# Layer norm's statistics of layer 0 worked out with tokens on partitions instead of on every partition

## The chip, the cores and the metric

The kernel runs on one core of a Trainium2 chip. The metric is the device time of one execution in microseconds (us). PE is the matrix engine, PEld its weight loads, DVE the vector engine, ACT the scalar engine, POOL the GpSimd engine, and SP issues DMAs.

## The reference

The input x is (2, 768, 64, 64) in float32. Two layers follow one another; the change touches layer 0 only, and in it only the layer norm over the 1536 channels of y.

```python
# layer 0
x_dbl = xs_seq @ x_proj_w.T                 # xs: in_proj, 3x3 depthwise conv, silu
dt, Bs, Cs = jnp.split(x_dbl, [R, R + DSTATE], axis=-1)
delta = softplus(einsum('blr,dr->bdl', dt, dt_w[0]) + dt_b)
# states: scan over tokens of dA = exp(delta * A), dBu = delta * u * Bs, 4 states a channel
y = jnp.einsum('bdln,bln->bdl', states, Cs) + D_param * u
mu = y.mean(-1, keepdims=True)
var = y.var(-1, keepdims=True)
y = (y - mu) * jax.lax.rsqrt(var + 1e-05) * ln_g + ln_b
out = y @ out_proj_w.T                      # then x = x + out
# layer 1: group norm, attention over statistics of w = x @ W_qkv.T, W_out, x = x + out
```

## The kernel before

Layer 0 keeps channels on partitions and tokens along the free dimension. The tokens of both images are cut into NCH = 16 chunks of N = 512 tokens (eight image rows each), and the 1536 channels into K = 12 tiles of P = 128. So there are NT = 192 pairs of chunk and tile. A loop over slots S = 0 to 213 is written out by hand for every engine: in slot S each engine does its share for tiles that entered the pipeline a fixed number of slots ago. A chunk takes 12 slots. In this document slots are counted modulo 12, so that in slot 8 the statistics of a chunk are worked out, and slot 0 is where a new chunk enters.

In slot S, PE multiplies tile S with the input weights (`in_proj`, L562, into bank p_in), and works on half of an output block of an older chunk (`out_proj`, L578, into bank p_op). In even slots it also sums y and y squared over channels with a matrix of ones (L633, L634, into the four quarters of p_ln). In every fourth slot it makes the inputs of softplus (`delta_pair`, L534, into p_dt), and in slots 1 and 2 the x_proj products (L667, also into p_dt). ACT moves p_in into the image window (L731), starts the convolution (L756), squares y (L762, which the sums of squares wait for) and writes the decays (L698) that DVE's scans need, two in the first half of a slot's work and two at the end of the slot before. DVE does four scans (L897), multiplies them by C (L907), adds six taps of the convolution (L922) and, in odd slots, scales and adds an output block (`scale_out` L929, `residual_add` L936, which sets s_ov and so lets PE use p_op again). POOL adds up and multiplies, and starts a DMA that adds two states onto two others (L851).

The order of the work on each engine is the order in which the loop's body issues it, and an engine goes on only when the wait at its head is met. Semaphores count: the name of the wait (s_ov, s_op, s_rstd, s_xd, s_delta, s_y) tells what is waited for. A matrix product of float32 with 512 columns shows as two passes in the trace.

For the norm, ACT copies the sums out of p_ln into LS at the end of slot 6 (L826): rows 0 to 63 hold the sums of squares, rows 64 to 127 the sums, each over 32 equal rows per quarter. At the end of slot 7, PE multiplies them with `pick`, a 128x128 matrix of one constant, so that the mean and the mean square of each token stand on all 128 partitions (L654, L656). In slot 8, ACT squares the mean (L744), DVE subtracts (L960) and adds epsilon (L962) between its first two times_c and its first tap, ACT takes Ln (L790) and Exp (L792) as a first guess of the root, and DVE does one Newton step in four operations after its last tap of the slot (L983, L985, L987, L989). All of these work on 128x512 values whose 128 rows are the same. The result RS is used by scale_out from slot 9 on. `norm_bank(c)` is p_dt, and p_da for the last chunk.

After the loop of the last chunk, PE still has two output blocks to do (`last_out_proj`, L608), DVE scales and adds the last six blocks (`scale_last`, `add_last`), and then layer 1 begins. The small operations of group norm (`group_norm_scale`, L66 to L101, values of 128x1) and layer 1's products with few columns (L1256) run on the same engines.

## Time and profile before

| | before |
|---|---|
| median of 3 runs (lowest to highest) | 3892.75 us (3892.51 to 3893.79) |
| the profiled execution: its time, its span | 3894.47 us, 3892.7 us |
| mean granted clock of PE, as a share of 2.4 GHz | 0.943 |
| PE busy, matrix products | 3479.1 us, 89% of the span, 10696 instructions |
| DVE busy | 2988.7 us, 77%, 4466 instructions |
| ACT busy | 2287.7 us, 59%, 3710 instructions |
| POOL busy | 2345.4 us, 60%, 1557 instructions |

Busy time is added over the whole span. Up to 81 us the kernel prepares weights and the first group norm; layer 0's loop runs from there to 2932 us, full from 484 us on; layer 1 takes the rest. An engine's share over the span therefore says little of any one stage. In the views, a bracket behind a row is the idle time of that engine just before it and the work that ended it.

### The profile page before, as it was taken

Reading aid. Unit: us, or ns where it says so; the run is one execution under the profiler, and the core shown is the slowest. Engines: PE = TensorE matmul, PEld = TensorE weight load, DVE = VectorE, ACT = ScalarE, POOL = GpSimd, SP = SyncE. Lnnn points to the kernel's source line nnn. Section 1 sums busy time; section 2 is a strip of 40 time slices with the busy share of each in tenths; the row PEclk is TensorE's granted clock in tenths of the full one; section 3 lists DMA queues with packets and bytes.
Section 4 is the critical chain, followed back from the end, with each engine's and each line's share of the span. In section 5 each row is a group of like instructions: output and inputs, shape, how many; then the busy total and the mean of one; then the engine's idle time right before and its main releaser. Section 6 shows DMA issues by size and latency. Waiting matters only on the chain. (4 is left out here: it accounts for less than half of the span.)

```text
span 3892.7 us, 39046 instructions
## 1 busy us (share of the span) xinstructions
PE 3479.1 (89%) x10696; PEld 1744.0 (45%) x10696; DVE 2988.7 (77%) x4466; ACT 2287.7 (59%) x3710; POOL 2345.4 (60%) x1557
## 2 busy tenths in 40 slices
PE   4875799999999899999989999998797999999999
PEld 4422233333333344333333333333245877767787
DVE  4459999999999979999999999999853345555532
ACT  1356767777777757776777777776534555432211
POOL 0138888888888868887888888888840001112211
PEclk7887899999999999999999999998898999999999
DMA  7234445545545544555555455554633223355654
GB/s 272 85 133 106 103 127 136 152 126 141 133 131 149 145 118 120 141 134 132 146 142 140 126 139 142 137 144 100 176 97 109 65 71 103 107 172 200 198 194 154
DMA packets 217034, 529.85 MB, mean 136 GB/s; under 512 B 24728, under 2 KB 45784, under 8 KB 213872
## 3 DMA queue, kind: packets, MB, share of 16 engines
q1 hardware_dynamic: 173808, 376.32, 30.5%
q0 software_dynamic: 43008, 151.02, 17.6%
q8 instruction: 88, 1.44, 0.1%
q14 instruction: 130, 1.06, 0.1%
HBM read 346.11 MB, written 80.48 MB: 110 GB/s over the span
## 5 line engine op out<-in xcount | busy, mean ns | idle before, releaser
L578 PE MATMUL p_op<-uy,wout_ring 128*128 128x512 f32 x2160 | 1060.0, 640 | 134.1 <-DVE x_res L936 134.0
L562 PE MATMUL p_in<-xn,win_v 128*128 128x512 f32 (+1 forms) x2304 | 1056.3, 609 | 76.7 <-ACT halo L735 43.4
L897 DVE TENSOR_TENSOR_SCAN p_da<-p_da,state,g_ring 128x512 f32<-128x512 f32 x672 | 827.3, 1277 | 121.2 <-ACT p_da L698 98.5
L869 POOL TENSOR_TENSOR g_ring<-du,B_bc 128x2048 f32<-128x2048 f32 x192 | 870.1, 4532 | 17.0 <-DMA B_bc<-bc_scratch 2.1
L922 DVE SCALAR_TENSOR_TENSOR p_cv<-win_v,conv_w,p_cv 128x512 f32<-128x512 f32 x960 | 722.9, 753 | 105.2 <-ACT p_cv L756 84.2
L578 PEld LDWEIGHTS p_op<-uy,wout_ring 128*128 128x128 f32 x2160 | 421.0, 203 | 771.3 <-issue 591.4
L562 PEld LDWEIGHTS p_in<-xn,win_v 128*128 128x128 f32 x2304 | 445.6, 197 | 657.4 <-issue 657.4
L698 ACT ACTIVATE p_da<-delta,A 128x512 f32<-128x512 f32 x768 | 496.8, 678 | 323.2 <-DVE g_ring L907 322.0
L907 DVE TENSOR_TENSOR g_ring<-p_da,C_bc 128x512 f32<-128x512 f32 x768 | 494.9, 686 | 1.1 <-issue 1.1
L1356 PE MATMUL banks<-x_split,w_split 128*128 128x512 f32 x1152 | 464.0, 403 | 24.9 <-DVE w_split L1536 19.7
L1358 PE MATMUL banks<-x_split,w_split 128*128 128x512 f32 x1152 | 451.7, 392 | 0.0
L1357 PE MATMUL banks<-x_split,w_split 128*128 128x512 f32 x1152 | 451.4, 392 | 0.0
L856 POOL TENSOR_TENSOR uy<-uy,conv_part 128x512 f32<-128x512 f32 x192 | 243.8, 1270 | 294.9 <-DVE uy L922 289.9
L1201 POOL DMA_DIRECT2D q_scratch<-q_ring x96 | 51.9, 540 | 537.5 <-DVE q_ring L1621 537.2
L851 POOL DMA_DIRECT2D g_ring<-g_ring x192 | 168.1, 876 | 193.3 <-DVE g_ring L907 185.0
L703 ACT ACTIVATE conv_part<-win_v,conv_w 128x512 f32<-128x512 f32 x384 | 274.1, 717 | 13.1 <-POOL uy L859 1.9
L1356 PEld LDWEIGHTS banks<-x_split,w_split 128*128 128x128 f32 x1152 | 217.7, 189 | 118.2 <-issue 39.4
L859 POOL TENSOR_TENSOR uy<-uy,conv_part 128x512 f32<-128x512 f32 x192 | 244.2, 1272 | 29.0 <-POOL uy L856 2.2
L877 POOL TENSOR_TENSOR uy<-uy,g_ring 128x512 f32<-128x512 f32 x192 | 243.8, 1270 | 15.1
L873 POOL TENSOR_TENSOR g_ring<-g_ring 128x512 f32<-128x512 f32 x192 | 243.8, 1270 | 10.8 <-DMA g_ring<-g_ring 10.8
L863 POOL TENSOR_TENSOR du<-delta,uy 128x512 f32<-128x512 f32 x192 | 248.5, 1294 | 2.0 <-ACT delta L717 2.0
L1358 PEld LDWEIGHTS banks<-x_split,w_split 128*128 128x128 f32 x1152 | 217.8, 189 | 47.4
(212 smaller groups left out, 4029.9 us busy)
## 6 DMA issues: line engine op xcount, KB each, us to landing
g_ring<-g_ring POOLq DMA_DIRECT2D x192, 512.0 KB, 5.2
win_v<-in_win SPq DMA_DIRECT2D x192, 384.0 KB, 3.2
wout_ring<-wout_scratch SPq DMA_DIRECT2D x184, 384.0 KB, 3.7
x_ring<-x_scratch SPq DMA_DIRECT2D x192, 256.0 KB, 2.7
q_scratch<-q_ring POOLq DMA_DIRECT2D x96, 256.0 KB, 2.4
x_split<-q_scratch SPq DMA_DIRECT2D x96, 256.0 KB, 3.2
out<-x_ring POOLq DMA_DIRECT2D x96, 256.0 KB, 2.8
x_res<-in_x SPq DMA_DIRECT2D x90, 256.0 KB, 4.2
```

The lines of the kernel that those rows point to most:

```text
L562: last = nc.tensor.matmul(p_in[:, 0:n], WR[:, i % NW, t, :], XN[:, t, off:off + n], start=(t == 0), stop=(t == XT - 1))
L578: last = nc.tensor.matmul(p_op[:], OR[:, e % NO, k - h * HALF, :], ucol(c * K + k), start=(k == 0), stop=(k == K - 1))
L698: nc.scalar.activation(p_da[:, n % 2, :], DL[:, i % ND, :], ACT.Exp, scale=At[:, j * NS + n:j * NS + n + 1]).then_inc(s_da, 1)
L703: nc.scalar.activation(rows(CT[:, n]), win_view(i, 2, 1 + n), ACT.Copy, scale=cwt[:, i % K, 7 + n:8 + n]).then_inc(s_ct, 1)
L863: nc.gpsimd.tensor_tensor(DU[:], DL[:, i % ND, :], ucol(i), ALU.mult).then_inc(s_du, 1)
L869: nc.gpsimd.tensor_tensor(G[:, i % NG], DU[:].unsqueeze(1).broadcast_to([P, NS, N]), BB[:], ALU.mult).then_inc(s_dbu, 1)
L897: nc.vector.tensor_tensor_scan(bank, bank, G[:, i % NG, n, :], init, ALU.mult, ALU.add)\
L907: nc.vector.tensor_tensor(G[:, i % NG, n], p_da[:, n % 2, :], CB[:, n], ALU.mult).then_inc(s_cm, 1)
L922: nc.vector.scalar_tensor_tensor(rows(dst), win_view(i, dy, dx), cwt[:, j, 3 * dy + dx:3 * dy + dx + 1], rows(p_cv[:]), ALU.mult, ALU.add) ...
L1356: nc.tensor.matmul(bank(m), WX[:, m, q, 0, :], hi(h), start=(q == 0), stop=False)
L1357: nc.tensor.matmul(bank(m), WX[:, m, q, 0, :], lo(h), start=False, stop=False)
L1358: last = nc.tensor.matmul(bank(m), WX[:, m, q, 1, :], hi(h), start=False, stop=(q == XT - 1))
```

## The change

The statistics are worked out with tokens on partitions. At the end of slot 7, PE now uses the sums LS as weights, 128 tokens at a time, and a `pick` of two columns as the moving operand: four products put the mean and the mean square of 512 tokens into 128x8 values. In slot 8, DVE copies them into `tst` (128 tokens by 4 blocks), squares, subtracts and adds epsilon in four operations; ACT takes Ln and Exp of 128x4; DVE does the four operations of the Newton step on 128x4, now ahead of the last three taps instead of behind them. At the end of slot 8, PE waits for the fourth of these and spreads the result: four products with `tst`'s column, repeated 128 times, as weights and the identity matrix `ident0` as moving operand write 1/sigma of 512 tokens to all 128 partitions. At the start of slot 9, ACT copies that into RS. ACT's Square is gone. `delta_pair` no longer waits for s_var. The identity matrix is loaded by one more DMA at the start, and `pick` is set by four small memsets instead of one.

```diff
-        pick = sb("pick", [P, P])
+        pick = sb("pick", [P, 2])
+        ident0 = sb("ident0", [P, P])
+        tst = sb("token_stats", [P, 8, N // P])
...
-                      (quad[:], g["quad_d"]), (fold[:], g["ident_d"]),
+                      (quad[:], g["quad_d"]), (fold[:], g["ident_d"]), (ident0[:], g["ident_d"]),
...
-                    wait(pe, s_var, norms_before(S))
                     wait(pe, s_rstd, norms_before(S))
...
-                        nc.tensor.matmul(norm_bank(c)[:, 0, :], pick[64:P, :], LS[64:P, :], start=True, stop=True)\
-                          .then_inc(s_mean, 1)
-                        nc.tensor.matmul(norm_bank(c)[:, 1, :], pick[0:64, :], LS[0:64, :], start=True, stop=True)\
-                          .then_inc(s_e2, 1)
+                        for tb in range(N // P):
+                            last = nc.tensor.matmul(norm_bank(c)[:, 0, 2 * tb:2 * tb + 2], LS[:, tb * P:(tb + 1) * P],
+                                                    pick[:], start=True, stop=True)
+                        last.then_inc(s_e2, 1)
+                    c = chunk_at(S, S_LN + 1)
+                    if c is not None:
+                        pe.wait_ge(s_nt, 4 * (c + 1))
+                        for tb in range(N // P):
+                            last = nc.tensor.matmul(norm_bank(c)[:, 1, tb * P:(tb + 1) * P],
+                                                    tst[:, 6, tb:tb + 1].broadcast_to([P, P]), ident0[:],
+                                                    start=True, stop=True)
+                        last.then_inc(s_rsb, 1)
...
-                    c = chunk_at(S, S_LN + 1)
+                    c = chunk_at(S, S_LN + 2)
                     if c is not None:
-                        act.wait_ge(s_mean, c + 1)
-                        act.wait_ge(s_e2, c + 1)
-                        nc.scalar.activation(LS[:], norm_bank(c)[:, 0, :], ACT.Square).then_inc(s_msq, 1)
+                        act.wait_ge(s_rsb, c + 1)
+                        wait(act, s_oa, XT * c)
+                        nc.scalar.activation(RS[:], norm_bank(c)[:, 1, :], ACT.Copy).then_inc(s_rstd, 1)
...
-                        nb = norm_bank(c)[:, 0, :]
-                        nc.scalar.activation(nb, LS[:], ACT.Ln).then_inc(s_lv, 1)
+                        nc.scalar.activation(tst[:, 4, :], tst[:, 3, :], ACT.Ln).then_inc(s_lv, 1)
                         act.wait_ge(s_lv, c + 1)
-                        nc.scalar.activation(nb, nb, ACT.Exp, scale=-0.5).then_inc(s_rs0, 1)
+                        nc.scalar.activation(tst[:, 4, :], tst[:, 4, :], ACT.Exp, scale=-0.5).then_inc(s_rs0, 1)
...
+                        st = norm_bank(c)[:, 0, 0:2 * (N // P)].rearrange("p (t s) -> p s t", s=2)
                         vec.wait_ge(s_e2, c + 1)
-                        vec.wait_ge(s_msq, c + 1)
-                        nb = norm_bank(c)
-                        nc.vector.tensor_tensor(nb[:, 1, :], nb[:, 1, :], LS[:], ALU.subtract).then_inc(s_var, 1)
-                        vec.wait_ge(s_var, c + 1)
-                        nc.vector.tensor_scalar(LS[:], nb[:, 1, :], 0.0, 1e-5, ALU.max, ALU.add).then_inc(s_vare, 1)
+                        nc.vector.tensor_copy(tst[:, 0:2, :], st).then_inc(s_var, 1)
+                        vec.wait_ge(s_var, 3 * c + 1)
+                        nc.vector.tensor_tensor(tst[:, 2, :], tst[:, 0, :], tst[:, 0, :], ALU.mult).then_inc(s_var, 1)
+                        vec.wait_ge(s_var, 3 * c + 2)
+                        nc.vector.tensor_tensor(tst[:, 2, :], tst[:, 1, :], tst[:, 2, :], ALU.subtract)\
+                          .then_inc(s_var, 1)
+                        vec.wait_ge(s_var, 3 * c + 3)
+                        nc.vector.tensor_scalar(tst[:, 3, :], tst[:, 2, :], 0.0, 1e-5, ALU.max, ALU.add)\
+                          .then_inc(s_vare, 1)
...
                         times_c(a, 2)
                         times_c(a, 3)
+                    c = chunk_at(S, S_LN + 1)
+                    if c is not None:
+                        vec.wait_ge(s_rs0, c + 1)
+                        nc.vector.tensor_tensor(tst[:, 5, :], tst[:, 4, :], tst[:, 3, :], ALU.mult).then_inc(s_nt, 1)
+                        vec.wait_ge(s_nt, 4 * c + 1)
+                        nc.vector.tensor_tensor(tst[:, 5, :], tst[:, 4, :], tst[:, 5, :], ALU.mult).then_inc(s_nt, 1)
+                        vec.wait_ge(s_nt, 4 * c + 2)
+                        nc.vector.tensor_scalar(tst[:, 5, :], tst[:, 5, :], -0.5, 1.5, ALU.mult, ALU.add)\
+                          .then_inc(s_nt, 1)
+                        vec.wait_ge(s_nt, 4 * c + 3)
+                        nc.vector.tensor_tensor(tst[:, 6, :], tst[:, 4, :], tst[:, 5, :], ALU.mult).then_inc(s_nt, 1)
                     if b is not None:
                         for n in range(3, len(TAPS)):
                             tap(b, n)
```

The four operations on 128x512 that stood behind these taps (L983 to L989) are removed.

## Rows read from the trace of the kernel before

**Rows 1.** Busy time by stretch: bounds, length, PE, PEld, DVE, ACT, POOL; clock, DMA.

```profile
484.00:2640.00 2156.00, 1991.07 (x5207) 796.95 (x5207) 1999.69 (x2800) 1548.37 (x2442) 1812.36 (x1099) 0.96 0.52 136
...
2786.00:2932.00 146.00, 132.97 (x340) 54.43 (x336) 93.61 (x138) 55.39 (x95) 78.74 (x45) 0.97 0.43 108
```

**Rows 2.** Waits of DVE and of PE, 484 to 2640: total us, times, longest.

```profile
DVE p_da L897 <- ACT p_da L698: 107.2, 49, 9.0
...
PE p_op L578 <- DVE x_res L936: 104.3, 45, 6.3
```

**Rows 3.** Timeline of DVE, 1656 to 1669, slot 8: start, duration, work.

```profile
1656.27 0.69 DVE L960 TENSOR_TENSOR p_dt<-p_dt,ln_sums 128x512 f32<-128x512 f32 x1
...
1657.60 2.33 DVE L922 SCALAR_TENSOR_TENSOR p_cv<-win_v,conv_w,p_cv 128x512 f32<-128x512 f32 x3
...
1662.29 1.29 DVE L907 TENSOR_TENSOR g_ring<-p_da,C_bc 128x512 f32<-128x512 f32 x2
...
1665.74 0.68 DVE L983 TENSOR_TENSOR ln_rstd<-p_dt,ln_sums 128x512 f32<-128x512 f32 x1
...
1668.52 1.22 DVE L897 TENSOR_TENSOR_SCAN p_da<-p_da,g_ring 128x512 f32<-128x512 f32 x1
```

**Rows 4.** Timeline of PE, 1650 to 1682, end of slot 7 to slot 9.

```profile
1651.91 0.69 PE L654 MATMUL p_dt<-ln_sums,pick 64*128 64x512 f32 x1
...
1652.97 5.42 PE L562 MATMUL p_in<-xn,win_v 128*128 128x512 f32 x12
...
1664.56 5.31 PE L562 MATMUL p_in<-xn,win_v 128*128 128x512 f32 x12
1673.71 7.11 PE L578 MATMUL p_op<-uy,wout_ring 128*128 128x512 f32 x12 [3.84 <-DVE x_res L936]
```

**Rows 5.** Timeline of PE: slot 11, slot 0, slot 9 at the images' edge.

```profile
523.57 4.54 PE L578 MATMUL p_op<-uy,wout_ring 128*128 128x512 f32 x6 [2.36 <-DVE x_res L936]
...
699.38 1.03 PE L633 MATMUL p_ln<-uy,ones 128*32 128x512 f32 x1 [3.13 <-ACT sq L762]
...
1505.78 5.42 PE L578 MATMUL p_op<-uy,wout_ring 128*128 128x512 f32 x12 [0.17 <-DVE x_res L936]
```

**Rows 6.** View of line 656: duration ns min/median/max, first and last start, forms.

```profile
L656 PEld LDWEIGHTS p_dt<-ln_sums,pick x30: 182/184/186, 477.7 to 2785.7; 64*128 64x128 f32 x30
```

**Rows 7.** Timelines: group norm's small steps, and products with few columns.

```profile
2937.55 0.20 ACT L101 ACTIVATE gtmp<-gtmp 128x1 f32<-128x1 f32 x1
2937.78 0.16 DVE L81 TENSOR_TENSOR gtmp<-gtmp 128x1 f32<-128x1 f32 x1 [1.28 <-ACT gtmp L101]
...
2938.56 0.21 DVE L89 TENSOR_SCALAR gbi<-gtmp,gsc 128x1 f32<-128x1 f32 x1
...
3322.60 0.95 PE L1256 MATMUL banks<-fsel,logits_t 128*128 128x12 f32 x8
```

**Rows 8.** Timeline of ACT and POOL, 1655 to 1685.

```profile
1657.95 0.58 ACT L790 ACTIVATE p_dt<-ln_sums 128x512 f32<-128x512 f32 x1
...
1680.21 0.88 POOL L851 DMA_DIRECT2D g_ring<-g_ring  x1 [3.16 <-DVE g_ring L907]
```

**Rows 9.** Busy time by slot, slots 9 to 2 of three chunks.

```profile
518.20:532.50 14.30, 11.38 (x25) 3.71 (x23) 13.34 (x20) 11.25 (x18) 12.40 (x9) 0.88 0.72 204
...
sum 81.30, PE 72.99 PEld 28.31 DVE 75.32 ACT 56.40 POOL 70.84; mean PE 12.17 PEld 4.72 DVE 12.55 ACT 9.40 POOL 11.81
...
sum 81.40, PE 72.47 PEld 28.18 DVE 75.33 ACT 56.66 POOL 70.83; mean PE 12.08 PEld 4.70 DVE 12.55 ACT 9.44 POOL 11.81
...
sum 80.10, PE 71.83 PEld 28.16 DVE 75.14 ACT 56.66 POOL 70.73; mean PE 11.97 PEld 4.69 DVE 12.52 ACT 9.44 POOL 11.79
```

**Rows 10.** Timeline of PE in the tail of layer 0.

```profile
2803.30 7.71 PE L578 MATMUL p_op<-uy,wout_ring 128*128 128x512 f32 x12 [5.31 <-DVE x_res L936]
...
2907.70 8.85 PE L608 MATMUL p_op<-uy,wout_ring 128*128 128x512 f32 x20 [0.53 <-DVE x_res L936]
```

**Rows 11.** Timeline of SP's DMA issues at the start.

```profile
4.17 0.43 SPq L213 DMA_DIRECT2D fold<-in_ident_d  x1
```

More of the change, by code:

```diff
@@ L232, in _ @@
                     nc.vector.memset(ones32[:], 1.0).then_inc(s_set, 1)
-                    nc.vector.memset(pick[:], 1.0 / (32 * DI)).then_inc(s_set, 1)
+                    nc.vector.memset(pick[0:64, 0:1], 0.0)
+                    nc.vector.memset(pick[0:64, 1:2], 1.0 / (32 * DI))
+                    nc.vector.memset(pick[64:P, 0:1], 1.0 / (32 * DI))
+                    nc.vector.memset(pick[64:P, 1:2], 0.0).then_inc(s_set, 1)
                     nc.vector.memset(xpt[:], 0.0).then_inc(s_set, 1)
@@ L327, in layer0 @@
          s_delta, s_du, s_dbu, s_da, s_scan, s_scp, s_cm, s_skip,
-         s_ns2, s_y, s_sq, s_ln, s_ls, s_mean, s_msq, s_e2, s_var, s_vare, s_lv, s_rs0, s_nt,
+         s_ns2, s_y, s_sq, s_ln, s_ls, s_rsb, s_e2, s_var, s_vare, s_lv, s_rs0, s_nt,
          s_rstd, s_op, s_ov, s_bn, s_pad, s_zero, s_oa, s_xe, s_xf, s_ct, s_conv) = (sem("q_" + n) for n in (
              "xn inp row rowev vev hin hout tap0 tap silu xp xd dt delta du dbu da "
-             "scan scp cm skip ns2 y sq ln ls mean msq e2 var vare lv rs0 nt rstd op ov bn pad "
+             "scan scp cm skip ns2 y sq ln ls rsb e2 var vare lv rs0 nt rstd op ov bn pad "
              "zero oa xe xf ct conv").split())
@@ L978, in _ @@
                             tap(b, n)
-                    c = chunk_at(S, S_LN + 1)
-                    if c is not None:
-                        vec.wait_ge(s_rs0, c + 1)
-                        nb = norm_bank(c)
-                        nc.vector.tensor_tensor(RS[:], nb[:, 0, :], LS[:], ALU.mult).then_inc(s_nt, 1)
-                        vec.wait_ge(s_nt, 3 * c + 1)
-                        nc.vector.tensor_tensor(nb[:, 1, :], nb[:, 0, :], RS[:], ALU.mult).then_inc(s_nt, 1)
-                        vec.wait_ge(s_nt, 3 * c + 2)
-                        nc.vector.tensor_scalar(LS[:], nb[:, 1, :], -0.5, 1.5, ALU.mult, ALU.add).then_inc(s_nt, 1)
-                        vec.wait_ge(s_nt, 3 * c + 3)
-                        nc.vector.tensor_tensor(RS[:], nb[:, 0, :], LS[:], ALU.mult).then_inc(s_rstd, 1)
                 def scale_last(r):
```

## The prediction

> **What bounds the kernel now.** The page's table of engines gives PE and DVE as the two busy ones over the span, which says nothing of a stage; so I read the table by stretch first. In the thirteen chunks of the steady part (484 to 2640) DVE is busy 2000 of 2156 us and PE 1991; from 2786 to 2932, the end of layer 0, DVE is busy 94 of 146 us and PE 133 [rows 1]. After 2932 comes layer 1, which the change leaves alone. So a gain must be made in layer 0's loop and can be lost in its tail.
>
> The waits in the steady part say who is late. DVE waits 107 us in 49 places, all before a scan whose decay ACT has not written; PE waits 104 us for the residual add (x_res) that frees bank p_op [rows 2]. The two engines take turns. The timelines show where: from slot 5 to slot 0 of the next chunk (slots counted modulo 12, as in the section on the kernel) DVE runs with hardly a gap and PE waits for it, at slot 9 by 3.84 us [rows 3, 4]; in slots 2 to 4, where x_proj, the fold and the delta products are added, I find no wait of PE, and there stand most of DVE's waits for decays. The statistics sit in slot 8, inside the stretch that DVE sets. What DVE is relieved of there moves everything up to slot 0, and PE starts its own critical stretch at an event that moves along: its wait for ACT's square in slot 0 (3.13 us [rows 5]). So a saving on DVE in slot 8 should shorten the period of a chunk, which is 164.9 us (14 periods between 477.7 and 2785.7 [rows 6]).
>
> **The change, part by part.** *DVE, removed.* The first two operations stand from 1656.27 to the next tap at 1657.60, 1.33 us; the last four from 1665.74 to the next scan at 1668.52, 2.78 us. DVE has no gap on either side. Removed: 4.11 us per chunk [rows 3].
>
> *DVE, added.* Eight operations on 128x4 or 128x8. Such shapes are not in the trace; the nearest are group norm's 128x1 steps, which depend on each other in the same way: L81 to L89 start at 2937.78 and 2938.56, four steps in 0.78 us, so 0.195 us each with the wait for the one before [rows 7]. Eight cost 1.56 us. The bounds: 0.16 each if they only take L81's own time, 1.3 us; 0.21 each, L89's, 1.7 us. Net saving 2.55 us per chunk (2.4 to 2.8).
>
> The Trainium skill (VectorE: DVE Perf Modes, the section on the TRN2 errata) warns against just this: an operation pays a fixed cost whatever its size, some 150 cycles, so many small ones lose. By it six large ones become eight small ones that are all fixed cost; an estimate from that page is 8 x 0.156 = 1.25 us, a saving of 2.86 us instead of 2.55. By that rule the small ones still win here, since each large one takes 0.68 us and more [rows 3].
>
> *ACT.* The Square goes, Ln and Exp shrink from 0.58 us (L790 [rows 8]) to 0.2 us each (L101 [rows 7]), and a copy of 128x512 from PSUM is added at the head of slot 9, about 0.6 us by L790's size. It waits for PE's spread, which ends near 1665.6; ACT's next task, the first tap, waits for DVE until about then anyway (DVE's last tap of slot 8 ends about where L983 begins, 1665.74 [rows 3]). DVE needs the copy at slot 9's scale_out, some 3.5 us after the scans begin. Cost nothing; if that cover were gone, the copy would delay the taps by its 0.6 us.
>
> *PE.* The two products with pick (four passes, two and two at once) take 1651.91 to 1652.97, 1.06 us [rows 4]. The four that replace them have 128x128 weights and two columns, two passes each: L1256 is the nearest, eight passes with 12 columns in 0.95 us [rows 7]. That is even. The spread adds eight passes of 128 columns with 128x128 weights. Lower bound L1256's 0.95 us; upper bound, weights and columns one after the other: 128 columns are a quarter of the 512 that take 0.53 us a pass (the two passes of 1651.91 [rows 4]), 0.13 each, so 8 x 0.13 more, 2.0 us. I take 1.0, by the row that it is nearest to. PE's wait of 3.84 us at slot 9 covers it: DVE comes 2.55 earlier and PE 1.0 later, which leaves about 0.3 us. In the one chunk at the edge between the images PE waits only 0.17 us there [rows 5], so that chunk gains nothing and may lose 0.5 us.
>
> *The new wait.* PE waits for the fourth Newton step (s_nt) before the spread, at the end of slot 8. Behind it stands everything of PE: in_proj of slot 9, and behind that ACT's evacuation. PE arrives after out_proj at 1664.5 [rows 4]. DVE's times_c ends at 1663.58 now [rows 3]; it moves 0.55 us earlier, since four small steps take the place of 1.33 us, and the four Newton steps add 0.78: 1663.8. The cover is 0.7 us. Ln and Exp, which stand between, run during the scans. I cost the wait at nothing; were the small steps 0.3 us each, it would be just reached.
>
> *POOL.* It waits 3.16 us for DVE before its DMA at 1680.21 [rows 8]; 2.55 of it go. POOL remains just covered.
>
> *The clock.* After PE's wait at slot 9 the granted clock falls to 1.2 GHz for part of the next products: twelve passes take 7.11 us at 1673.71 instead of the 5.42 at 1652.97 [rows 4]. With the wait nearly closed, I expect the full 2.4 GHz in slot 9. PE then reaches slot 11 earlier and waits there instead. The first chunk of the trace shows that pattern already: a wait of 2.36 us at slot 11 [rows 5] and a mean clock of 0.88 in that slot, which takes 14.3 us [rows 9]. Its six slots 9 to 2 sum to 81.3 us; two other chunks give 81.4 and 80.1 [rows 9], and the rest mix these two kinds, about 80.7 on average (my estimate, half of each). If all chunks take the first one's form, this costs 0.6 us of each chunk's gain. Bounds: nothing, and the 1.2 between 81.3 and 80.1.
>
> *The tail.* For the last chunk the order is a loss. Now PE goes from pick's products to last_out_proj at 2907.70 after a wait of 0.53 us [rows 10]. New: the statistics wait for DVE's residual add as well, which ends just before 2907.70; four steps to 2908.4, Ln and Exp to 2908.9, four steps to 2909.7, spread to 2910.7, and only then the last products, on which the end of layer 0 hangs. That is 3.0 us, and 2.7 us of idle before it may bring the lower clock, 1.7 us more, as at 1673.71 [rows 4]. I take 4.5 (3 to 6). The chunk before it keeps its gain, since PE still waits 5.31 us for DVE at 2803.30 [rows 10].
>
> *The start.* One more DMA before the loads of x: the issue of fold took 0.43 us [rows 11], plus its gap 0.5 us, straight on the path.
>
> **Sum.** Fourteen chunks x (2.55 - 0.6) = 27.3; less 0.5 at the image edge, 4.5 in the tail and 0.5 at the start: 21.8 us. The profiled execution took 3894.5 us (span 3892.7), 1.7 above the median of 3892.75; a difference carries over, so 3871.
>
> **Rivals.** (a) *The forecast*, 3871; with its bounds, 14 x 2.84 - 3.5 = 36 us at best (3857), 14 x (2.4 - 1.2) - 7.5 = 9 us at worst (3884). Chance 0.68.
> (b) *The clock gives more.* With slot 9 closed, the waits at 11 and 0 may be too short to lower it. Then each chunk saves up to the 1.3 us between the 81.4 and the 80.1 on top, say 14 x (2.7 + 1.3) - 4 = 52 us: 3841. For it: PE loses 1.7 us in slot 9 now. Against: PE's idle is moved rather than removed, and the wait of 3.13 us in slot 0 remains. Chance 0.09. The Trainium skill (TensorE: Matmul & The Clock Gate, on HAM oscillation) speaks for it: a loop in which PE idles each time pays the slower clock each time. The trace agrees, with 7.11 us for what takes 5.42.
> (c) *PE absorbs it.* If the spread costs 2.0 us and the statistics products do not run as closely as L1256, PE is late at slot 9 by 1 us or more, and the delta products of slot 11 and ACT's softplus bring this back to DVE; a chunk gains 0.3 and the tail takes it: 3892 (no change). For it: DVE already waits 107 us for ACT. Against: PE has 2.4 us at slot 11 and 3 at slot 0 to recover. Chance 0.15.
> (d) *Slower*: the wait for s_nt. If the Newton steps end late, because Ln and Exp stand on ACT behind decays that wait for times_c, PE stands at the head of slot 9. It loses 0.7 us of cover first, then the 0.3 of slot 9, then what slots 11 and 0 give; it decides once the steps come more than about 4 us after times_c. At 5 us each chunk loses 1: 14 + 5 = 19 us, 3912. Against: ACT runs Ln now at 1657.95, 5 us before the end of times_c [rows 8]. Chance 0.08.
>
> **Numbers.** The likeliest is (a), 3871. Range 3852 to 3892: it takes in (a) with its bounds, the near part of (b) and most of (c), and leaves out 0.06 of (b), some 0.04 of (c) and (d), 0.18 in all. A run of this kernel tells about 0.2% (7.8 us) from no change. Faster: nearly all of (a) and (b), and a little of (c), 0.79. Within 0.2%: most of (c), a bit of (a), 0.13. Slower 0.08.
>
> **What would show it.** The eight small steps at 0.195 us from start to start; slot 8 shorter by 2.5 us; PE's wait for x_res at slot 9 below 1 us and the clock there 1.0; a new wait at slot 11; no wait of PE on s_nt except in the last chunk, where it is 2 to 3 us; 14 shorter periods of about 163. It is wrong if PE waits at the spread in every chunk, if small steps take 0.3 us or more, or if DVE's waits for decays grow by what it saved.

## The result and the profile after

The changed kernel took 3921.51 us (median of 4 runs, 3915.42 to 3923.51), the kernel before 3892.63 us on the same chip. The ratio is 1.0071 with a 95% interval of 1.0053 to 1.0088: slower by 29 us, where the forecast was 22 us faster. The profiled execution took 3920.41 us, its span is 25.9 us longer, and the mean granted clock is 0.944 against 0.943. Every ratio below is to the kernel before, run beside the variant on the same chip (medians 3889.2 to 3891.0 us); the variants ran on three chips. Two of e12's ten executions, at 4562 and 7948 us, fell in a slower state and are left out of its median.

The table of busy time by stretch of the changed kernel answers to [rows 1]. DVE is busy 3.7 us more in the steady part instead of less, PE 10 us less:

```profile
484.00:2640.00 2156.00, 1980.77 (x5305) 817.53 (x5304) 2003.37 (x2800) 1518.08 (x2420) 1793.88 (x1088) 0.96 0.52 135
2786.00:2932.00 146.00, 131.74 (x355) 54.84 (x354) 98.19 (x144) 59.29 (x98) 100.47 (x58) 0.96 0.48 115
```

The view of waits, same stretch, answers to [rows 2]. DVE waits for decays as before (L908 is the old L897). PE's 104 us for the residual add are now 65, and 51 us at the spread (L666) are new, 3.9 us in each of 13 chunks. ACT waits for the clamp (L977):

```profile
DVE p_da L908 <- ACT p_da L710: 104.8, 48, 7.5
...
PE p_op L582 <- DVE x_res L947: 64.9, 36, 3.6
...
ACT token_stats L801 <- DVE token_stats L977: 56.5, 13, 4.7
PE p_dt L666 <- DVE token_stats L1002: 51.3, 13, 4.9
```

So something ahead of the spread is late. The timeline of DVE in slot 8 of the chunk of [rows 3] shows it. Columns: start, duration, work.

```profile
1663.81 1.29 DVE L918 TENSOR_TENSOR g_ring<-p_da,C_bc 128x512 f32<-128x512 f32 x2
1665.02 0.15 DVE L970 COPY token_stats<-p_dt 128x8 f32<-128x8 f32 x1
1665.21 3.91 DVE L972 TENSOR_TENSOR token_stats<-token_stats 128x4 f32<-128x4 f32 x1
1669.15 1.19 DVE L974 TENSOR_TENSOR token_stats<-token_stats 128x4 f32<-128x4 f32 x1
1670.37 0.17 DVE L977 TENSOR_SCALAR token_stats<-token_stats 128x4 f32<-128x4 f32 x1
```

The square of four values per partition takes 3.91 us and the subtraction 1.19, while the copy ahead of them takes 0.15 and the clamp behind them 0.17. The timeline of POOL, same moment:

```profile
1664.58 4.52 POOL L880 TENSOR_TENSOR g_ring<-du,B_bc 128x2048 f32<-128x2048 f32 x1
1669.06 1.26 POOL L884 TENSOR_TENSOR g_ring<-g_ring 128x512 f32<-128x512 f32 x1
1670.40 1.27 POOL L888 TENSOR_TENSOR uy<-uy,g_ring 128x512 f32<-128x512 f32 x1
```

The square ends at 1669.12, POOL's long product (L880) at 1669.10; the subtraction ends at 1670.34, POOL's next at 1670.32. Both DVE operations end 0.02 us after the POOL operation that ran when they started. The view of the tile `token_stats` (minimum, median, maximum in ns) shows that this is the rule, that the Newton step (L995 on) mostly escapes it (L1002 was caught once, 2.00 us), and that the clamp was caught once:

```profile
L972 DVE TENSOR_TENSOR token_stats<-token_stats x16: 161/3928/4073, 479.5 to 2930.9; 128x4 f32<-128x4 f32 x16
L974 DVE TENSOR_TENSOR token_stats<-token_stats x16: 161/1186/1198, 479.7 to 2931.1; 128x4 f32<-128x4 f32 x16
L977 DVE TENSOR_SCALAR token_stats<-token_stats x16: 170/170/4378, 479.9 to 2931.3; 128x4 f32<-128x4 f32 x16
L995 DVE TENSOR_TENSOR token_stats<-token_stats x16: 151/153/164, 490.2 to 2932.0; 128x4 f32<-128x4 f32 x16
```

The timeline of PE answers to [rows 4]. The statistics products cost 0.95 us, as forecast; the spread waits 4.05 us, and after that wait it runs at a granted clock of 0.50, which is 1.2 GHz (2.08 us):

```profile
1660.56 0.95 PE L659 MATMUL p_dt<-pick,ln_sums 128*128 128x2 f32 x8
...
1677.15 2.08 PE L666 MATMUL p_dt<-ident,token_stats 128*128 128x128 f32 x8 [4.05 <-DVE token_stats L1002]
```

The kernel before held the same thing in a row that I had not read. Its group norm steps at 382 us work on the same 128x1 tile as the ones I took my 0.195 us from [rows 7], but POOL is busy there. Timelines of DVE and of POOL, kernel before:

```profile
381.94 1.26 DVE L72 TENSOR_TENSOR gtmp<-gtmp 128x1 f32<-128x1 f32 x1
...
383.43 4.34 DVE L76 TENSOR_TENSOR gtmp<-gtmp 128x1 f32<-128x1 f32 x1
```

```profile
381.92 1.26 POOL L863 TENSOR_TENSOR du<-delta,uy 128x512 f32<-128x512 f32 x1
383.26 4.49 POOL L869 TENSOR_TENSOR g_ring<-du,B_bc 128x2048 f32<-128x2048 f32 x1
```

4.34 us for one value per partition, ending at 387.77 with POOL's 387.75.

**Where the 26 us are.** Three lengths read from each kernel's trace: slot 8 on DVE (from its first scan to that of slot 9, median), 14 chunk periods (from the first chunk's statistics products on PE to the fifteenth's), and the time within these 14 at the granted clock of 1.2 GHz.

| kernel | slot 8 | 14 periods | at 1.2 GHz |
|---|---|---|---|
| before | 16.16 | 2308.0 | 205 |
| after | 18.17 | 2331.9 | 205 |
| e1, one operand in PSUM | 13.38 | 2257.0 | 123 |
| e12, e1 with 3 fills | 15.13 | 2289.5 | 143 |
| e6, e1 with 6 fills | 16.83 | 2306.4 | 167 |
| e10, e1 with the spread twice | 13.38 | 2267.1 | 143 |

The loop gives 23.9 of the 25.9 us: slot 8 is 2.0 us longer in most chunks, 26.7 us over the fourteen, of which 3 are given back in the other slots. PE's new wait is thus what DVE's longer slot does to PE, and not a second loss beside it.

### The profile page after: what moved, and what is told of

It reads as the page before. It is cut to its first block and busy times, and to the rows that moved or that the text cites. A ratio compares the mean times of both kernels' runs of the same rounds, so it can differ in the third digit from the quotient of the medians.

```text
span 3918.6 us, 39363 instructions
## 1 busy us (share of the span) xinstructions
PE 3487.5 (89%) x10888; PEld 1778.3 (45%) x10888; DVE 3012.7 (77%) x4501; ACT 2270.9 (58%) x3710; POOL 2345.3 (60%) x1557
## 5 line engine op out<-in xcount | busy, mean ns | idle before, releaser
L566 PE MATMUL p_in<-xn,win_v 128*128 128x512 f32 (+1 forms) x2304 | 1073.9, 617 | 77.1 <-ACT halo L747 43.2
L582 PE MATMUL p_op<-uy,wout_ring 128*128 128x512 f32 x2160 | 1036.7, 628 | 92.9 <-DVE x_res L947 92.9
L908 DVE TENSOR_TENSOR_SCAN p_da<-p_da,state,g_ring 128x512 f32<-128x512 f32 x672 | 827.3, 1277 | 121.8 <-ACT p_da L710 99.0
L880 POOL TENSOR_TENSOR g_ring<-du,B_bc 128x2048 f32<-128x2048 f32 x192 | 869.9, 4531 | 16.5 <-DMA B_bc<-bc_scratch 1.6
L1372 PEld LDWEIGHTS banks<-x_split,w_split 128*128 128x128 f32 x1152 | 217.4, 189 | 117.3 <-issue 38.1
L743 ACT ACTIVATE win_v<-p_in 128x512 f32<-128x512 f32 (+1 forms) x192 | 111.9, 583 | 226.2 <-PE p_in L566 226.2
```

The source lines that it names most:

```text
L566: last = nc.tensor.matmul(p_in[:, 0:n], WR[:, i % NW, t, :], XN[:, t, off:off + n], start=(t == 0), stop=(t == XT - 1))
L582: last = nc.tensor.matmul(p_op[:], OR[:, e % NO, k - h * HALF, :], ucol(c * K + k), start=(k == 0), stop=(k == K - 1))
L880: nc.gpsimd.tensor_tensor(G[:, i % NG], DU[:].unsqueeze(1).broadcast_to([P, NS, N]), BB[:], ALU.mult).then_inc(s_dbu, 1)
L908: nc.vector.tensor_tensor_scan(bank, bank, G[:, i % NG, n, :], init, ALU.mult, ALU.add)\
L1372: nc.tensor.matmul(bank(m), WX[:, m, q, 0, :], hi(h), start=(q == 0), stop=False)
```

## The experiments

Theory A: an elementwise operation of DVE whose operands all lie in SBUF cannot run beside an operation of POOL and waits for its end. The Trainium skill (SBUF — State Buffer, "SBUF: two separate sides") has a rule close to it, and narrower: DVE with two SBUF inputs, or in a mode that reads through two ports, and GpSimd take one shared pair of ports as an exclusive lock; the first holds it for its whole instruction, and the other is blocked until it is free. The trace agrees, with 3.91 us for what takes 0.16 alone.

### e1: the same arithmetic with one operand in PSUM

```diff
+        def pst(c):
+            return norm_bank(c)[:, 0, 64:64 + 8 * (N // P)].rearrange("p (s t) -> p s t", t=N // P)
...
-                        nc.vector.tensor_tensor(tst[:, 2, :], tst[:, 0, :], tst[:, 0, :], ALU.mult).then_inc(s_var, 1)
+                        nc.vector.tensor_tensor(pst(c)[:, 2, :], st[:, 0, :], tst[:, 0, :], ALU.mult).then_inc(s_var, 1)
...
-                        nc.vector.tensor_tensor(tst[:, 2, :], tst[:, 1, :], tst[:, 2, :], ALU.subtract)\
+                        nc.vector.tensor_tensor(pst(c)[:, 3, :], tst[:, 1, :], pst(c)[:, 2, :], ALU.subtract)\
```

and so on for the clamp, Ln, Exp and the Newton step. ACT's two results thus lie in PSUM as well.

> The changed kernel, with one operand of each small DVE operation in PSUM (squared mean, variance, guess and Newton's product lie in the bank of the statistics), same places in the order, same semaphores. Theory A (a small operation with all operands in SBUF is held up while POOL's operation runs; in the changed kernel the first product takes 3.9 us and the next 1.2, and both end with POOL's operation): all eight take 0.15 to 0.2 us, slot 8 of DVE falls from 18.2 to 13.6 us, PE's wait of about 4 us at the spread goes, 14 x 4.55 = 64 us less than the changed kernel at most; with the pattern of slot 11 of the first chunk, 3862 to 3873. Rival B (small chained operations are slow in themselves when DVE comes from long ones): the times of 3.9 and 1.2 us stay, 3921. Rival C (the loss is PE's, from the spread and its wait at the head of slot 9): DVE becomes fast and the kernel stays above 3893.

Measured: 3840.24 us (3837.59 to 3843.77), ratio to before 0.9869 [0.9854, 0.9884], faster by 49 us. The view of the tile, kernel e1:

```profile
L975 DVE TENSOR_TENSOR p_dt<-p_dt,token_stats x15: 170/170/171, 481.1 to 2739.8; 128x4 f32<-128x4 f32 x15
L977 DVE TENSOR_TENSOR p_dt<-token_stats,p_dt x15: 166/166/167, 481.3 to 2740.0; 128x4 f32<-128x4 f32 x15
```

No small operation takes more than 0.171 us, whatever POOL does. The durations are as theory A has them, and B and C fall. The time is 22 us below its range; e6 and e12 ask why.

### e2, e3, e4: one small product more in the kernel before

One 128x4 product per chunk, its result unused. e2: both sources in SBUF, ahead of L960, where POOL is busy. e3: same place, first source in PSUM. e4: e2's product behind the fourth scan of slot 9, where POOL is idle.

```diff
+                        nc.vector.tensor_tensor(dmy[:], pick[:, 0:4], pick[:, 4:8], ALU.mult).then_inc(s_var, 1)    # e2
+                        nc.vector.tensor_tensor(dmy[:], nb[:, 0, 0:4], pick[:, 4:8], ALU.mult).then_inc(s_var, 1)   # e3
                         nc.vector.tensor_tensor(nb[:, 1, :], nb[:, 1, :], LS[:], ALU.subtract).then_inc(s_var, 1)
```

> The kernel before, with one more DVE product of 128x4 values once a chunk, both sources and the result in SBUF, just ahead of the subtraction in slot 8 (in the trace of before: at 1656.27, when POOL's long product runs from 1655.83 to 1660.38). Theory A: it ends with POOL's product, so it takes about 4 us, and each of 14 chunks is about 4 us longer: 3893 + 14 x 4.1 = 3950 (3940 to 3955). Rival B (a cost of small operations as such, here a single one, not chained): at most 0.2 us, 3893 to 3896.

> As the run before it, but the first source of the added product is in PSUM (four columns of the mean). Theory A: 0.16 to 0.2 us although POOL's product runs, 3893 to 3897. If any small operation beside a POOL operation is held up, whatever its operands: 4 us, 3950.

> As the first of the two, both sources in SBUF, but placed behind the fourth scan of slot 9, where POOL waits (in the trace of before POOL is idle from 1677.05 to 1680.21 and the place is at 1678.2). Theory A: 0.16 to 0.2 us, 3893 to 3897. If the operands alone make it slow, without POOL: about 4 us, 3950.

Measured: e2 3924.7 us, ratio 1.0082 [1.0062, 1.0102]; e3 3892.89, 1.0006 [0.9996, 1.0015]; e4 3895.95, 1.0013 [1.0003, 1.0022]. The view of the added line in e2, e3 and e4, in this order:

```profile
L961 DVE TENSOR_TENSOR dmy_out<-pick x16: 164/4136/4350, 485.5 to 2947.9; 128x4 f32<-128x4 f32 x16
```

```profile
L961 DVE TENSOR_TENSOR dmy_out<-p_dt,pick x15: 152/152/153, 481.6 to 2791.4; 128x4 f32<-128x4 f32 x15
```

```profile
L976 DVE TENSOR_TENSOR dmy_out<-pick x16: 151/153/153, 502.2 to 2917.8; 128x4 f32<-128x4 f32 x16
```

The same instruction costs 4.1 us or 0.15, by its place alone (e2, e4) and by one operand alone (e2, e3). Its end in e2 is POOL's end: timelines of DVE and POOL, kernel e2, 993.70 against 993.68.

```profile
989.53 4.17 DVE L961 TENSOR_TENSOR dmy_out<-pick 128x4 f32<-128x4 f32 x1
```

```profile
989.15 4.53 POOL L870 TENSOR_TENSOR g_ring<-du,B_bc 128x2048 f32<-128x2048 f32 x1
```

POOL's product takes 4.53 us with DVE waiting, as it does without: DVE, which came second, pays all. e2 was expected at 3940 to 3955 and came lower. Slot 8 is 4.1 us longer in most chunks, but 49 us over the fourteen and not 57, since in two of them only a short operation of POOL runs at the product's place; the 14 periods are longer by only 32.6 us (2340.6). The other 16 are given back in slots 1 to 3: in a late chunk slots 1 and 2 take 13.4 and 14.3 us, where the kernel before takes up to 14.7 and 16.0.

### e5: only the square gets its operand from PSUM

```diff
-                        nc.vector.tensor_tensor(tst[:, 2, :], tst[:, 0, :], tst[:, 0, :], ALU.mult).then_inc(s_var, 1)
+                        nc.vector.tensor_tensor(tst[:, 2, :], st[:, 0, :], tst[:, 0, :], ALU.mult).then_inc(s_var, 1)
```

> The changed kernel, where only the first of its 128x4 products (the square of the mean, line 972) takes one source from PSUM; the subtraction, the clamp and the Newton step keep SBUF operands. Theory A (an elementwise DVE operation with all operands in SBUF can't run beside a POOL operation and waits for its end): the product takes about 0.15 us, and the subtraction behind it now starts about 4 us before the end of the long POOL operation and takes the 4 us in its place; the time stays that of the changed kernel, 3912 to 3926 us. Rival B (the product is slow by itself, because it is the first SBUF-only operation after the scans): 3838 to 3860 us, with every small operation under 0.3 us. Rival C (each SBUF-only operation adds its own part): half way, 3870 to 3900 us.

Measured: 3923.2 us (3922.69 to 3928.8), ratio 1.0079 [1.0062, 1.0096], as theory A said. Timeline of DVE, kernel e5:

```profile
644.21 0.16 DVE L972 TENSOR_TENSOR token_stats<-p_dt,token_stats 128x4 f32<-128x4 f32 x1
644.40 3.72 DVE L974 TENSOR_TENSOR token_stats<-token_stats 128x4 f32<-128x4 f32 x1
648.16 1.20 DVE L977 TENSOR_SCALAR token_stats<-token_stats 128x4 f32<-128x4 f32 x1
```

The wait passes to the next operation. Mending the row that looks slow gains nothing; every operation in reach of POOL's product must be mended.

### e8 and e9: which operations are held

e8 puts a one-source operation in the place of e2's product. e9 puts four forms one behind the other into e1.

```diff
+                        nc.vector.tensor_scalar(dmy[:], pick[:, 0:4], 2.0, 1.0, ALU.mult, ALU.add).then_inc(s_var, 1)   # e8
...
+                        nc.vector.tensor_reduce(dmy[:, 0:1], ident0[:, 0:4], AX.X, ALU.add).then_inc(s_var, 1)          # e9
+                        nc.vector.tensor_tensor(norm_bank(c)[:, 0, 96:100], ident0[:, 0:4], ident0[:, 4:8], ALU.mult).then_inc(s_var, 1)
+                        nc.vector.tensor_copy(dmy[:, 4:8], ident0[:, 4:8]).then_inc(s_var, 1)
+                        nc.vector.scalar_tensor_tensor(dmy[:, 8:12], ident0[:, 0:4], Dp[:, 0:1], ident0[:, 4:8], ALU.mult, ALU.add).then_inc(s_var, 1)
```

> The kernel before plus one 128x4 TENSOR_SCALAR from SBUF to SBUF (one source, multiply and add with constants) per chunk on DVE, at the place where the SBUF-only product of e2 took 4.1 us. Theory A1 (an SBUF-only operation is blocked whatever the number of its sources): it takes about 4 us and the time is 3915 to 3929 us, as in e2. Theory A2 (only two SBUF sources block): it takes 0.16 us, and the time is that of before, 3886 to 3897 us; the one clamp of 4.38 us in the changed kernel would then need another reason.

> The kernel of e1 with four more small DVE operations per chunk, ahead of the copy of the sums, while the 4.5 us POOL operation and two of 1.26 us behind it run. All read SBUF alone: a TENSOR_REDUCE to SBUF (one source), a TENSOR_TENSOR of two sources into PSUM, a COPY to SBUF (one source), a SCALAR_TENSOR_TENSOR of two sources to SBUF. An operation that is not held takes 0.15 to 0.2 us and leaves the POOL operation running for the next; one that is held takes what is left of the POOL operation (about 4 us the first, about 1.2 us each one behind it). Theory A1 (what counts is that no operand is in PSUM): reduce 4, product into PSUM 0.16, copy 1.2, scalar-tensor-tensor 1.2, time 3900 to 3930 us. Theory A3 (what counts is the sources, wherever the result goes): the product into PSUM is held too. Theory A4 (only two sources, or the one-source forms that run with a wider access, are held): the reduce is free, copy and scalar-tensor-tensor are held.

Measured: e8 3924.42 us, ratio 1.0072 [1.005, 1.0094]; the view of its line:

```profile
L961 DVE TENSOR_SCALAR dmy_out<-pick x16: 170/4167/4410, 474.5 to 2929.4; 128x4 f32<-128x4 f32 x16
```

One source is enough for this form. e9 took 3902.68 us (3899.0 to 3905.8). Timelines of DVE and POOL, kernel e9:

```profile
644.98 0.15 DVE L974 TENSOR_REDUCE dmy_out<-ident 128x1 f32<-128x4 f32 x1
645.04 4.06 DVE L975 TENSOR_TENSOR p_dt<-ident 128x4 f32<-128x4 f32 x1
649.02 0.16 DVE L976 COPY dmy_out<-ident 128x4 f32<-128x4 f32 x1
649.09 1.23 DVE L977 SCALAR_TENSOR_TENSOR dmy_out<-ident,cols 128x4 f32<-128x4 f32 x1
```

```profile
644.55 4.53 POOL L884 TENSOR_TENSOR g_ring<-du,B_bc 128x2048 f32<-128x2048 f32 x1
649.03 1.27 POOL L888 TENSOR_TENSOR g_ring<-g_ring 128x512 f32<-128x512 f32 x1
```

The reduction runs in the middle of POOL's product and is free: theory A1 ("all in SBUF") falls. (So does layer 0's BATCH_NORM_STATS2, whose one source of 128x512 is in SBUF: in the kernel before it took 0.68 us beside an operation of POOL 21 times of 22, and ended 0.2 us ahead of it.) The product with two SBUF sources is held though its result goes to PSUM (A3), and so is the scalar-tensor-tensor. So it is the sources that count; with e8, theory A stands in this form: two SBUF sources, or the one-source TENSOR_SCALAR; not a reduction. Why the one form with one source is held and the other not, no run here shows. The copy stays open: it started 0.06 us before POOL's product ended and took 0.16, in between two POOL operations, so it was never tried against one.

### e11: SBUF operands, but moved behind POOL's products

The copy, square, subtraction and clamp stand behind the last scans of slot 8, directly ahead of the Newton step; no operand is changed.

```diff
                         times_c(a, 2)
                         times_c(a, 3)
                     c = chunk_at(S, S_LN + 1)
                     if c is not None:
+                        vec.wait_ge(s_e2, c + 1)
+                        nc.vector.tensor_copy(tst[:, 0:2, :], st).then_inc(s_var, 1)
...
                         vec.wait_ge(s_rs0, c + 1)
```

> The changed kernel with SBUF operands as they are, but its first four small DVE operations (copy, square, subtraction, clamp) stand behind the last scans of slot 8, directly ahead of the Newton step, where POOL is idle for some 4 us. Theory A: every small operation takes 0.15 to 0.21 us, slot 8 of DVE is 13.4 us plus some 0.5 us of wait for ACT's root, and the time is 3840 to 3860 us, more if ACT, which now waits for the clamp some 5 us longer, delays its evacuations. Rival B (the square and the subtraction are slow by themselves at their first use in a chunk): they take 3.9 and 1.2 us here too, 3915 us or more.

Measured: 3880.28 us (3872.64 to 3885.18), ratio 0.9978 [0.9969, 0.9988]: the square has a median of 0.49 us instead of 3.93 and the subtraction 0.16 instead of 1.19, so rival B falls, but the time misses the 3840 to 3860 expected. Slot 8 takes 14.5 us, 1.1 more than in e1. The timeline of DVE in two chunks of e11 shows why:

```profile
652.49 0.54 DVE L985 TENSOR_TENSOR token_stats<-token_stats 128x4 f32<-128x4 f32 x1
...
654.04 0.16 DVE L993 TENSOR_TENSOR token_stats<-token_stats 128x4 f32<-128x4 f32 x1 [0.51 <-ACT token_stats L803]
...
2768.44 2.02 DVE L990 TENSOR_SCALAR token_stats<-token_stats 128x4 f32<-128x4 f32 x1
2770.97 4.05 DVE L993 TENSOR_TENSOR token_stats<-token_stats 128x4 f32<-128x4 f32 x1 [0.51 <-ACT token_stats L803]
```

0.51 us go to the wait for Exp, and 0.38 to the end of POOL's last product. In the chunk before the last the order of the slots differs, POOL is busy in this place too, and two operations take 6.1 us; that slot lasts 17.6 us, against 9.0 in e1. The fourteen slots 8 ahead of it are 16.5 us longer than in e1 and this one 8.6, together 25 of the 31.4 us by which the profiled span is longer. A place where POOL is idle helps as long as it stays idle; an operand in PSUM helped in every chunk here.

### e6, e12: e1 made as long as before

Why is e1 faster by 49 us, when 22 were forecast with about the same DVE time saved? e6 fills e1's slot 8 with six MEMSETs of 128x416 in PSUM ahead of the copy of the sums, e12 with three.

```diff
+                        for n in range(6):
+                            nc.vector.memset(norm_bank(c)[:, 0, 96:512], 0.0).then_inc(s_var, 1)
+                            vec.wait_ge(s_var, 9 * c + 1 + n)
```

> The kernel of e1 (small operations with one operand in PSUM), with six fills of 128x416 values in PSUM on DVE ahead of the copy of the sums in slot 8, an estimated 6 x 0.47 = 2.8 us, which makes slot 8 on DVE as long as it was in the kernel before (16.2 against 13.4 us). Theory D1 (all of the gain of e1 beyond the forecast comes from DVE's shorter slot, and what TensorE's clock gives back follows from it): the time comes back to that of before, 3884 to 3894 us. Theory D2 (part of it comes from TensorE's own work, whose stretch of wait in slot 9 has gone together with the wide sum over the partitions): 3855 to 3878 us, and no TensorE wait of 3.8 us in slot 9.

> The kernel of e1 with three of the six fills of e6, which took 0.57 us each with their gaps: slot 8 of DVE 15.1 us, between 13.4 (e1, 3840 us) and 16.8 (e6, 3904 us). Theory L (TensorE's clock follows DVE's length evenly, so that each microsecond of slot 8 costs about 1.4 us of time per chunk): 3868 to 3876 us. Rival K (the clock's share comes in one step, with TensorE's wait in slot 9 that only the shortest slot removes): 3878 to 3890 us; or with its wait in slot 8 that only the longest slot brings: 3858 to 3866 us.

Measured: e6 3904.36 us (3900.25 to 3908.34), ratio 1.0035 [1.0024, 1.0046]; e12 3879.95 us, ratio 0.9971 [0.996, 0.9981]. A fill took 0.41 us and 0.57 with its gap, so e6 is 3.4 us longer than e1 in slot 8 and not 2.8, which puts it above its expectation. By the table, the first 1.75 us of fills cost 32.5 us over 14 chunks, 1.33 us for each microsecond of them; the next 1.70 cost 16.9, 0.71 for each. At the slot length of before (16.16) the line between the two gives 2299.7. So of e1's 51.0 us over 14 periods about 43 come with DVE's length and about 8 with the rest of the change, TensorE's and ACT's part of it, which no run takes apart. That is D1 for the larger part, though e6's time lies in neither range. Where the 51.0 lie on DVE says the same in another way: the slots 8 are shorter by 39.3 us, and 11.7 more are saved elsewhere (slots 1 to 3 shorter by 15.2, slot 11 longer by 4.1). e12's time is where rival K has it, but not for its reason: PE's wait in slot 9 is 0.9 us in a late chunk of e1 and 1.1 in e12, and the time at 1.2 GHz rises evenly, 123, 143, 167 us. Why the first fills cost more than their own length stays open.

### e10: the spread twice

```diff
-                        for tb in range(N // P):
+                        for tb in [t for t in range(N // P)] + [t for t in range(N // P)]:
```

> The kernel of e1, but TensorE does each chunk's spread of the root twice (8 more 128x128 passes, 1.05 to 2.08 us by the traces). Theory of the forecast (DVE's slots set the pace, TensorE waits for them and absorbs what it does more): 3838 to 3848 us. Rival (TensorE limits as well in the slots 8 and 9): each chunk is longer by the passes, 3856 to 3870 us.

Measured: 3849.97 us (3849.58 to 3851.31), 10 us more than e1: 0.7 us per chunk, between the two expectations. Two rows of PE's timeline, e1 first and e10 second, show the price of eight passes at full clock (granted 1.00 in both rows), 1.95 less 1.16 us:

```profile
1641.50 1.16 PE L669 MATMUL p_dt<-ident,token_stats 128*128 128x128 f32 x8
```

```profile
1642.77 1.95 PE L669 MATMUL p_dt<-ident,token_stats 128*128 128x128 f32 x16
```

So TensorE absorbs next to nothing of it, although its wait in slot 9 (0.9 us in e1) closes. DVE's slots 8 and 9 are unchanged, 13.4 us each; what is longer in the chunks with the changed pattern are slots 1 and 2 (14.6 and 16.0 us, against 13.4 and 14.3), with 6.8 us at 1.2 GHz in slot 0.

### e7: e1 with the tail mended

For the last chunk the spread comes after the first half of the last output projection.

```diff
                 def last_out_proj(m):
                     for h in range(2):
+                        if m == 4 and h == 1:
+                            spread(CL)
```

> The kernel of e1, but for the last chunk TensorE spreads the root after the first half of the last output projection instead of before it. Theory of the forecast (the wait for the root and the slower restart cost 4.5 us at the end of layer 0): 3.5 to 4.5 us less than e1 in the stretch from the end of the last residual to the end of layer 0, so about 3834 to 3838 us. Rival: DVE's six last scalings and additions then end last (they start some 3 us later), and nothing or under 1 us is gained.

Measured: 3838.93 us (3838.48 to 3840.45), ratio 0.9859 [0.9841, 0.9878], 52 us under before. The intervals of e1 and e7 overlap and their medians are 1.3 us apart, so the times alone do not tell the two; the traces do. Timeline of PE, kernel e7:

```profile
2854.40 5.42 PE L625 MATMUL p_op<-uy,wout_ring 128*128 128x512 f32 x12 [0.80 <-DVE x_res L955]
2859.66 1.05 PE L613 MATMUL p_da<-ident,token_stats 128*128 128x128 f32 x8
2860.55 5.32 PE L625 MATMUL p_op<-uy,wout_ring 128*128 128x512 f32 x12
```

From the last Newton step to the end of the projections it takes 19.9 us, e1 23.5; the 14 periods are alike (2257.1, 2257.0), and the span is 3.3 us shorter, a little less than the 3.5 to 4.5 expected.

## Why the prediction was wrong, point by point

**The step that failed** is the term of DVE's added work: "Eight operations on 128x4 or 128x8 ... 0.195 us each", with its upper bound of 0.21. The eight take 6.1 us in the chunk shown (0.15, 3.91, 1.19, 0.17 and four of 0.16), not 1.56. I took the price from steps of the same form at 2937 us, after layer 0, where POOL does nothing, and carried it to a place where POOL is busy without a gap. What decides the price is what POOL does and where the sources lie (e1 to e5, e8, e9). Net of the 4.11 us removed, slot 8 is 2.0 us longer instead of 2.55 shorter; [rows 3] had shown no such wait, since each of the removed operations has a source in p_dt.

**The page of the Trainium skill that I weighed** (VectorE: DVE Perf Modes, the TRN2 errata) was about the fixed cost of small operations. It agrees with the runs, 0.15 to 0.17 us each, and was beside the point. I wrote that the small ones "still win": true of e1, not of this change.

**DVE, with the wait gone.** e1 shortens slot 8 by 2.78 us; the term was 2.55 (2.4 to 2.8). Right.

**PE.** The statistics products cost 0.95 us, as taken. The spread takes 1.16 us in e1, against the 1.0 taken. "DVE comes 2.55 earlier and PE 1.0 later, which leaves about 0.3 us" held in e1: 0.9 us of wait in most late chunks. But cover at slot 9 did not make the spread free: e10 puts 0.7 us per chunk on eight passes.

**The new wait.** I costed PE's wait for s_nt at nothing and named it as rival (d) with another cause, Ln and Exp late on ACT. It came, at 3.9 us in each of 13 chunks, because the clamp ahead of them was late on DVE; ACT waited 4.3 us on average for it. PE's idle time moved from slot 9 into slot 8, and the lower clock with it: 205 us at 1.2 GHz in both kernels.

**The clock.** I took 0.6 us per chunk as a loss. e1 shows the other sign: with the same DVE length it is 8 us better than before, and its time at 1.2 GHz falls from 205 to 123 us. In the five periods from 1629 to 2431 us a chunk takes 160.3 to 160.6 us, with 3.4 us at 1.2 GHz in slot 7 and nowhere else. The waits at slots 11 and 0 are still there (2.4 and 3.1 us) and no longer bring it down. That was rival (b)'s 3841, and e1 took 3840, but (b) as I told it gave the change itself this time, which it never had. The Trainium skill (TensorE: Matmul & The Clock Gate, on HAM oscillation) describes a loop whose idle stretch is paid for anew in every round; here the same two waits are followed by the lower clock in some chunks of e1 and not in others, so the trace agrees in part only, and the rule gives no count of what a shorter wait wins.

**The tail.** 4.5 us forecast. The changed kernel starts the last projections 3.5 us after the last residual add, and after 2.75 us of idle time it runs them at the lower clock for a part (11.61 us for the 24 passes that took 10.57 before). Together 4.5. Timeline of PE, kernel after, beside [rows 10]:

```profile
2932.81 1.73 PE L666 MATMUL p_da<-ident,token_stats 128*128 128x128 f32 x8 [2.75 <-DVE token_stats L1002]
2934.33 11.61 PE L612 MATMUL p_op<-uy,wout_ring 128*128 128x512 f32 x24
```

e7 takes 3.3 of it back. The small steps are at 0.16 us there, where POOL is idle.

**The sums.** Three slips change nothing: the best case uses 2.84 us a chunk where the bound says 2.8; the worst takes off 7.5 us where its terms give 7.0 (6 in the tail, 0.5 at the edge, 0.5 at the start); the tail's parts add to 4.7 where 4.5 was taken.

**The chances.** Slower had 0.08, for one mechanism that decides at 4 us of delay. The delay was there; I looked for it on ACT and not in the duration of the new operations. The view of the tile `gtmp` in the kernel before would have said it, with a maximum of 4344 ns beside a median of 159:

```profile
L76 DVE TENSOR_TENSOR gtmp<-gtmp x4: 159/159/4344, 78.3 to 2988.2; 128x1 f32<-128x1 f32 x4
```

## What to carry to other kernels

Before pricing a small DVE operation by a row, look at what POOL does at that row and at the place where it is to go, and at the maximum beside the median: a product with two SBUF sources, or a scalar operation from SBUF to SBUF, that starts while POOL computes lasts until POOL's operation ends, however small it is. Keep one source in PSUM where the data can lie there, which costs next to nothing here (0.17 us against 0.16) and turned a loss of 29 us into a gain of 49; it must be done for every such operation in reach, since mending the first hands the wait to the next. When DVE and TensorE take turns, do not book cover as free: 0.8 us more of TensorE beside a wait of 0.9 still cost 0.7 per chunk.

## What the runs showed that was not expected

- A DVE operation on four values per partition took 0.15 to 4.4 us, and its end followed that of POOL's operation by 0.02 us. POOL's own 4.53 us did not change.
- A TENSOR_REDUCE with one SBUF source was not held (0.15 us in the middle of POOL's product), a TENSOR_SCALAR with one SBUF source was (median 4.17 us).
- The same waits of PE, 2.4 us in slot 11 and 3.1 in slot 0, are followed by 1.2 GHz in some chunks of e1 and not in others. Timeline of PE, kernel e1, two chunks:

```profile
847.47 2.84 PE L585 MATMUL p_op<-uy,wout_ring 128*128 128x512 f32 x6 [2.35 <-DVE x_res L950]
...
857.27 1.03 PE L640 MATMUL p_ln<-uy,ones 128*32 128x512 f32 x1 [3.12 <-ACT sq L777]
...
1994.75 2.84 PE L585 MATMUL p_op<-uy,wout_ring 128*128 128x512 f32 x6 [2.36 <-DVE x_res L950]
...
2004.55 0.59 PE L640 MATMUL p_ln<-uy,ones 128*32 128x512 f32 x1 [3.12 <-ACT sq L777]
```

  The granted clock is 0.50 from 856.3 to 863.1 us and 1.00 throughout 1994.7 to 2017; the chunk takes 163.3 us in the one case and 160.5 in the other. What decides between them no run here settles.
